# A decoder's l0 feed-forward prepared in one block, and its l1 selective scan laid out on 128 lanes

## The reference

```python
def _reorder_quantize_x(x, idx):                      # layer 0, feed-forward
    scale = jnp.max(jnp.abs(x)) / GLOBAL_DIV
    xr = (x / scale)[:, idx]
    scale_x = jnp.max(jnp.abs(xr), axis=1, keepdims=True) / FP8_MAX
    return (_fp8(xr / scale_x), scale_x, scale)
def _qlinear(qx, scale_x, scale, W, idx):
    Wr = W[:, idx]
    w_scale = jnp.max(jnp.abs(Wr), axis=1, keepdims=True) / FP8_MAX
    return qx * scale_x @ (_fp8(Wr / w_scale) * w_scale).T * scale
...
delta = jax.nn.softplus(delta_r @ dt_proj_W.T + dt_proj_b) * 0.001   # layer 1, attention
delta_A = jnp.exp(jnp.einsum('bld,dn->bldn', delta, A))               # n: 16 states, d: 96 channels
delta_B_u = jnp.einsum('bld,bln,bld->bldn', delta, Bp, u)
x = dA_t * x + dBu_t                                                  # over the 256 steps
y = jnp.einsum('bdn,bn->bd', x, C_t)                                  # ... + u * Dp
```

## Time and profile before

| | us |
|---|---|
| median of 3 runs (2959.87 to 2961.27) | 2960.64 |
| the profiled execution | 2961.07 |
| its span, first to last instruction | 2959.2 |
| l0 feed-forward, preparation (three blocks) | from 284 to 403.2 |
| l0 feed-forward, 8 tiles | 403.2 to 494.3 |
| layernorm ahead of l1 attention | 494.3 to 503.3 |
| l1 attention up to the scan | 503.3 to 578.1 |
| l1 scan and y out of PSUM | 578.1 to 704.1 |

### The profile page before, as it was taken

The page is one execution under the profiler, slowest core; times in us unless marked ns, Lnnn a source line. Parts: engine busy times, 40 slices in busy tenths (PEclk is TensorE's granted clock), DMA queues, the critical chain, the costliest instruction groups (busy, mean ns, idle before and its releaser), DMA issues. The chain is left out here.

```text
span 2959.2 us, 37118 instructions
## 1 busy us (share of the span) xinstructions
PE 2425.8 (82%) x14074; PEld 1610.9 (54%) x14074; DVE 1737.1 (59%) x3519; ACT 1008.2 (34%) x2293; POOL 769.9 (26%) x573
## 2 busy tenths in 40 slices
PE   7797343486999997977979797889998887999899
PEld 4555222123434555665858586755557765555555
DVE  5435678696435664278696969525665763565311
ACT  3032001362105552124545453415552131555210
POOL 1120001000007883300000000008881000888322
PEclk8788555697999998987888989789999969999999
DMA  1000000003000001041010101030001004000311
GB/s 35 19 21 22 0 0 14 0 0 107 1 0 1 1 1 58 1 147 27 30 29 30 29 30 29 2 100 1 1 1 43 21 1 100 1 1 1 118 36 39
DMA packets 98937, 81.29 MB, mean 27 GB/s; under 512 B 51504, under 2 KB 90272, under 8 KB 98185
## 3 DMA queue, kind: packets, MB, share of 16 engines
q1 hardware_dynamic: 97737, 77.47, 9.2%
q0 software_dynamic: 1024, 1.45, 0.2%
HBM read 73.56 MB, written 5.35 MB: 27 GB/s over the span
## 5 line engine op out<-in xcount | busy, mean ns | idle before, releaser
L2017 POOL TENSOR_SCALAR work<-work,small 128x512 f32<-128x512 f32 x384 | 594.3, 1566 | 706.6 <-DVE small L1952 705.3
L1995 ACT ACTIVATE work<-psum,small 128x512 f32<-128x512 f32 x384 | 260.6, 683 | 254.6 <-DVE small L1947 254.6
L1947 DVE TENSOR_REDUCE small<-psum 128x2 f32<-128x1024 f32 x192 | 234.7, 1224 | 176.0 <-PE psum L1897 176.0
L1907 PEld LDWEIGHTS psum<-consts,work 128*128 128x128 f32 x1536 | 165.4, 141 | 113.8 <-issue 102.1
L1897 PE MATMUL psum<-keysT,arena_a 64*128 64x512 f32 x768 | 219.2, 650 | 8.9 <-ACT work L1995 6.0
L1919 PE MATMUL psum<-work,keys 128*64 128x256 f32 x1536 | 187.0, 384 | 36.9 <-issue 34.3
L1907 PE MATMUL psum<-consts,work 128*128 128x128 f32 x1536 | 211.3, 281 | 3.5 <-DVE work L1958 2.6
L1919 PEld LDWEIGHTS psum<-work,keys 128*64 128x64 f32 x1536 | 120.0, 136 | 136.7 <-issue 110.8
L2849 PE MATMUL psum<-xnT,arena_a 128*128 128x256 f32 x512 | 138.2, 425 | 24.7 <-DVE arena_b L3269 23.8
L1958 DVE COPY work<-psum 128x512 f32<-128x512 f32 x192 | 130.9, 682 | 19.7 <-PE psum L1907 19.7
L2002 ACT ACTIVATE work<-psum 128x512 f32<-128x512 f32 x192 | 114.4, 596 | 71.8 <-PE psum L1907 71.8
(11 more groups left out here) (589 smaller groups left out, 4992.5 us busy)
## 6 DMA issues: line engine op xcount, KB each, us to landing
arena_b<-alpha_rows SPq DMA_DIRECT2D x16, 512.0 KB, 5.7
arena_a<-in_L_xattn_Wo SPq DMA_DIRECT2D x3, 2048.0 KB, 14.6
arena_a<-in_L_xattn_Wq SPq DMA_DIRECT2D x3, 2048.0 KB, 12.7
arena_a<-in_L_xattn_w_kc_q SPq DMA_DIRECT2D x3, 1536.0 KB, 12.2
arena_a<-in_L_attn_w_qkv SPq DMA_DIRECT2D x1, 4096.0 KB
arena_a<-in_L_xattn_W_qr SPq DMA_DIRECT2D x3, 768.0 KB
arena_b<-in_L_ffn_w_fc SPq DMA_DIRECT2D x1, 2048.0 KB
arena_b<-in_L_ffn_w_proj SPq DMA_DIRECT2D x1, 2048.0 KB
```

Source lines behind the costliest of these rows:

```text
L1907: mm = nc.tensor.transpose(ps[:, 4 + j, c * P:(c + 1) * P], probs[u % NPB][:, j, c * P:(c + 1) * P], k.c["ident"])
L1947: nc.vector.tensor_reduce(top[:, 2 * u:2 * u + 2], ps[:, u % 2 * 2:u % 2 * 2 + 2, :], AX.X, ALU.max, negate=True).then_inc(*maxed.up())
L1995: nc.scalar.activation(probs[u % NPB][:, j, :], ps[:, u % 2 * 2 + j, :], ACT.Exp, bias=top[:, i:i + 1], accum_out=total[:, i:i + 1]).then_ ...
L2017: nc.gpsimd.tensor_scalar(probs[u % NPB][:, j, :], probs[u % NPB][:, j, :], total[:, i:i + 1], None, ALU.mult).then_inc(*scaled.up())
```

## The change

In `l0_ffn` the first three blocks become one. The input is masked, reduced and rounded by DVE in the same instruction list as the weights, behind the weights' rounding. The row scales are spread by PE right after DVE has made them, into banks 3 to 7, and ACT copies them out. The permutation runs in two halves (`half`), each of 8 gate/up and 32 down matmuls, and ACT copies out both halves. The transposed and permuted input is copied out half by DVE and half by ACT. In the block over tiles `scale(t + 1)` now stands ahead of `hidden(t)`, the residual of a tile comes one turn later behind its hidden rows instead of two, and PE takes up the transposes of a tile two turns later.

In `l1_attn` the arrays of the step size and of the scan go from 96 partitions x 1024 to 128 partitions x (3 x 256): each batch has 32 partitions (`lane(b)`), and the 96 channels are three groups `j` of 32. `u` is brought into this layout by 12 transfers within the on-chip memory (`own_u`), and the three per-channel vectors and tables are loaded four times each, once for each batch. Operations with a per-partition scalar are issued once for each `j`. PE writes to 32 partitions at a time: `spread` has 8 matmuls of 256 columns per state (for 4 of 512) and `collect` 12 blocks of 32 x 32 (for 2 matmuls of 96 x 96), which also bring the sum back to 96 partitions.

```diff
...
             for i in range(4):
-                dve.wait_ge(*mm.at(1))
                 c, g = divmod(i, 2)
-                nc.vector.tensor_copy(qguT[:, c, g * F:(g + 1) * F], ps[:, 3 + i, :].bitcast(BF16)[:, 0:F])
+                last = nc.vector.tensor_copy(qguT[:, c, g * F:(g + 1) * F], ps[:, 3 + i, :].bitcast(BF16)[:, 0:F])
+            last.then_inc(*taken.up())
...
+            nc.vector.reciprocal(rx, sx).then_inc(*taken.up())
+            dve.wait_ge(*taken.at(2))
+            k.link(dve, nc.vector.tensor_scalar(rx, rx, FP8_MAX, None, ALU.mult), "dve")
+            k.link(dve, nc.vector.tensor_scalar(sx, sx, 1.0 / FP8_MAX, None, ALU.mult), "dve")
+            k.link(dve, nc.vector.tensor_tensor(xm, xm, rx.unsqueeze(2).broadcast_to([P, NT, D]), ALU.mult), "dve")
+            quantise(k, dve, xm, xt, qx)
+            nc.vector.tensor_copy(rx, rx).then_inc(*prep.up())
+            dve.wait_ge(*turned.at(1))
+            nc.vector.tensor_copy(qxT[:, 0, :], ps[:, 4, :].bitcast(BF16)).then_inc(*taken.up())
+            dve.wait_ge(*mm.at(6))
+            nc.vector.tensor_copy(xpick[:, 0, :].rearrange("p (a b) -> p a b", a=2), ps[:, 6:8, :])
...
+        @block.scalar
+        def _(act):
+            act.wait_ge(*rows_done.at(1))
             for i in range(4):
-                nc.vector.tensor_copy(scale_row[:, i * F // 2:(i + 1) * F // 2], ps[:, 4 + i, 0:F // 2])
+                nc.scalar.activation(scale_row[:, i * F // 2:(i + 1) * F // 2], ps[:, 4 + i, 0:F // 2], ACT.Copy)
+            nc.scalar.activation(scale_row2, ps[:, 3, 0:D], ACT.Copy).then_inc(*taken_act.up())
+            for half in range(2):
+                act.wait_ge(*mm.at(2 + 2 * half))
+                nc.scalar.activation(wpick[:, half, :].rearrange("p (a b) -> p a b", a=4), ps[:, 4:8, 0:F // 2],
+                                     ACT.Copy).then_inc(*taken_act.up())
+                act.wait_ge(*mm.at(3 + 2 * half))
+                nc.scalar.activation(wd_pick[:, 4 * half:4 * half + 4, :].rearrange("p (a b) d -> p a (b d)", a=2),
+                                     ps[0:FP, 2 * half:2 * half + 2, :], ACT.Copy)
+            act.wait_ge(*turned.at(2))
+            nc.scalar.activation(qxT[:, 1, :], ps[:, 5, :].bitcast(BF16), ACT.Copy).then_inc(*taken_act.up())
+            act.wait_ge(*mm.at(7))
+            nc.scalar.activation(xpick[:, 1, :].rearrange("p (a b) -> p a b", a=2), ps[:, 4:6, :], ACT.Copy)
...
             m.then_inc(*counted.up())
+            pe.wait_ge(*prep.at(2))
+            for t in range(16):
+                nc.tensor.matmul(ps[:, 4 + t // 4, t % 4 * FP:(t % 4 + 1) * FP], k.c["ones"][0:FP, :],
+                                 column(t, FP), start=True, stop=True)
+            for t in range(2):
+                m = nc.tensor.matmul(ps[:, 3, t * P:(t + 1) * P], k.c["ones"], column(16 + t, P), start=True, stop=True)
+            m.then_inc(*rows_done.up())
             pe.wait_ge(*prep.at(3))
+            pe.wait_ge(*taken_act.at(1))
...
+            for half in range(2):
+                pe.wait_ge(*(taken.at(1) if half == 0 else taken_act.at(2)))
...
+                m.then_inc(*mm.up())
+                if half == 0:
+                    pe.wait_ge(*taken.at(2))
+                for j in range(4 * half, 4 * half + 4):
+                    for t in range(FT):
+                        m = nc.tensor.matmul(ps[0:FP, j // 2, j % 2 * D:(j % 2 + 1) * D], pick_down[:, t, j * FP:(j + 1) * FP],
+                                             qdT[:, t, :], start=t == 0, stop=t == FT - 1)
+                m.then_inc(*mm.up())
+            pe.wait_ge(*prep.at(4))
+            pe.wait_ge(*taken_act.at(3))
...
-                if t >= 1:
-                    u = t - 1
+                if t >= 2:
+                    u = t - 2
...
-            for t in range(NT + 2):
+            scale(0)
+            for t in range(NT + 1):
+                if t + 1 < NT:
+                    scale(t + 1)
                 if t < NT:
-                    scale(t)
                     hidden(t)
-                if t >= 2:
-                    residual(t - 2)
+                if t >= 1:
+                    residual(t - 1)
...
+    G, J = P // B, C * B // P
...
-                                (cols[:, 0:1], col("L1_attn_conv_b", C)), (cols[:, 1:2], col("L1_attn_dt_proj_b", C)),
-                                (cols[:, 2:3], col("L1_attn_D_param", C)), (a_log, io["L1_attn_A_log"])])
+                                (conv_b, col("L1_attn_conv_b", C))]
+                 + [pair for b in range(B) for pair in (
+                     (a_log[lane(b)], io["L1_attn_A_log"].rearrange("(j g) n -> g j n", g=G)),
+                     (dt_b[lane(b)], col("L1_attn_dt_proj_b", G)), (skip[lane(b)], col("L1_attn_D_param", G)))])
...
-            nc.vector.tensor_scalar(conv.rearrange("p (a b) -> p a b", a=2), ps[0:C, 0:2, :], cols[:, 1:2], None,
-                                    ALU.add).then_inc(*k.sig("z").up())
+            for j in range(J):
+                last = nc.vector.tensor_scalar(z[:, j, :], ps[:, j // 2, j % 2 * S:(j % 2 + 1) * S], dt_b[:, j:j + 1], None, ALU.add)
+            last.then_inc(*k.sig("z").up())
...
-            nc.vector.tensor_tensor(du, delta, u, ALU.mult)
-            nc.vector.tensor_scalar(hC[1], u, cols[:, 2:3], None, ALU.mult)
+            dve.wait_ge(*laned.at(16 * B * J))
+            nc.vector.tensor_tensor(du, delta, own_u, ALU.mult)
+            for j in range(J):
+                nc.vector.tensor_scalar(hC[1][:, j, :], own_u[:, j, :], skip[:, j:j + 1], None, ALU.mult)
+
+        @block.sync
+        def _(sp):
+            sp.wait_ge(*silued.at(1))
+            for b in range(B):
+                for j in range(J):
+                    sp.dma_start(own_u[lane(b), j, :], u[G * j:G * j + G, b * S:(b + 1) * S]).then_inc(*laned.up(16))
...
-            for n in range(2):
-                mm = nc.tensor.matmul(ps[0:C, n, :], w_dt, low[:, n * 512:(n + 1) * 512], start=True, stop=True)
+            for j in range(J):
+                for b in range(B):
+                    mm = nc.tensor.matmul(ps[lane(b), j // 2, j % 2 * S:(j % 2 + 1) * S], w_dt[:, G * j:G * j + G],
+                                          low[:, b * S:(b + 1) * S], start=True, stop=True)
...
+            def spread(s):
+                if s >= 4:
+                    pe.wait_ge(*read.at(s - 3))
+                for g in range(2):
+                    at = R + g * NS + s
+                    for b in range(B):
+                        mm = nc.tensor.matmul(ps[lane(b), s % 4, g * S:(g + 1) * S], w_x[:, at:at + 1].broadcast_to([C, G]),
+                                              u[:, b * S:(b + 1) * S], start=True, stop=True)
                 mm.then_inc(*bred.up())
 
...
+                for d in range(B):
+                    for j in range(J):
+                        b = (j + d) % B
+                        mm = nc.tensor.matmul(ps[G * j:G * j + G, 4 + b, 0:S],
+                                              k.c["ident"][lane(b), lane(b)], hC[s % 2][lane(b), j, :],
+                                              start=s < 0, stop=s == NS - 1, skip_group_check=True)
...
-                k.link(act, nc.scalar.activation(dA[s % 2], delta, ACT.Exp, scale=a_log[:, s:s + 1]), "act")
-                nc.scalar.activation(ln_dA[s % 2], dA[s % 2], ACT.Ln, bias=k.c["tiny"][0:C]).then_inc(*decay.up())
+                for j in range(J):
+                    last = nc.scalar.activation(dA[s % 2][:, j, :], delta[:, j, :], ACT.Exp, scale=a_log[:, j, s:s + 1])
+                k.link(act, last, "act")
+                nc.scalar.activation(ln_dA[s % 2], dA[s % 2], ACT.Ln, bias=k.c["tiny"]).then_inc(*decay.up())
 
...
-                nc.vector.tensor_tensor(two(dBu[s % 2]), two(du), ps[0:C, b_at, :], ALU.mult).then_inc(*taken.up())
+                row = lambda g: ps[:, s % 4, g * S:(g + 1) * S].unsqueeze(1).broadcast_to([P, J, S])
+                dve.wait_ge(*bred.at(s + 1))
+                nc.vector.tensor_tensor(dBu[s % 2], du, row(0), ALU.mult).then_inc(*taken.up())
                 dve.wait_ge(*decay.at(s + 1))
-                k.link(dve, refine_exp(k, dve, dA[s % 2], delta, a_log[:, s:s + 1], ln_dA[s % 2]), "dve")
+                for j in range(J):
+                    own = ln_dA[s % 2][:, j, :]
+                    last = nc.vector.scalar_tensor_tensor(out=own, in0=delta[:, j, :], scalar=a_log[:, j, s:s + 1], in1=own,
+                                                          op0=ALU.mult, op1=ALU.subtract)
+                k.link(dve, last, "dve")
+                k.link(dve, nc.vector.scalar_tensor_tensor(out=dA[s % 2], in0=ln_dA[s % 2], scalar=1.0, in1=dA[s % 2],
+                                                           op0=ALU.add, op1=ALU.mult), "dve")
                 dve.wait_ge(*taken.at(s + 1))
-                for b in range(B):
...
+                for j in range(J):
```

(3 more changed lines are left out.)

144 lines of the change are left out of this document (39 added, 105 removed).

## The result

The changed kernel takes 2888.61 us (median of 4 runs, 2887.71 to 2889.92), the kernel before 2960.26 beside it (2958.35 to 2961.27). The ratio is 0.9758, with a 95% interval of 0.9744 to 0.9772: 71.7 us less, where 60.7 were forecast. The profiled execution took 2889.24 us, its span is 2887.4.

The account below looks back on a forecast made before the run. DVE was taken as the bound in l1_attn and the PE/DVE hand-over in l0_ffn's preparation. Terms -32.2 - 3.5 + 4.2 - 7.0 - 22.2 = -60.7 us gave a median of 2900.0, range 2888 to 2914.

Parts of the forecast that it names:

- l0 preparation: In l0_ffn ahead of the tiles: hand-over waits between PE and DVE go, first tile's matmul at 371.0, 32 us less.
- half of 3.86 us: In the l0 preparation: PE's time for each gate/up half, within 17.7 us for both halves of the permutation.
- by the row the sum stands: In the l0 preparation: PE's clock stays at 0.50 as in the old row, so the halves take 17.7 us.
- the first rival: TensorE's clock rises in the merged l0 block: 9 us less, 2891; chance 8%.
- Tiles: l0 tile loop: the 0.85 us tanh waits go, two new waits come; 3.5 us less.
- Loads: Layernorm ahead of l1: nine more loads issued by SP put all engines 4.2 us back; bound 7.5 us.
- l1 ahead of the scan: l1_attn before the scan: rows shrink from 1024 to 768 elements, and the w_dt product shortens; 7.0 us less.
- Scan: l1_attn scan: a step falls from 7.30 to 5.91 us, 22.2 us less over 16.
- the second rival: In the scan: ACT or PE becomes the bound, or short instructions cost more; 2917 or 2942; chance 13%.
- The last sum: End of the scan: the last collect, in the open, costs the same 3.4 us as now; bounds 0.9 to 10.2.
- The slower rival: In the scan: collect's 24 instructions go strictly one after another at 1.2 GHz, 11.9 us a step, 2996; chance 4%.
- the likeliest case: Whole kernel: the forecast schedule, median 2900.0, alone ranging from 2893 to 2909; the forecast keeps 75%.

Follow-up runs that it names:

- e7_by_rows: The changed kernel with the 12 blocks of each collect issued batch by batch instead of along diagonals; 2888.66 us, ratio 0.9758.
- late loads: The changed kernel with l1 attention's twelve per-lane loads issued in the next block; 2891.31 us, ratio 0.9745, and again 2884.53 us, ratio 0.9748.
- e2_l1_only: The new l1_attn with the old l0_ffn, against the kernel before; 2930.43 us, ratio 0.9909.
- e5_before_fill: The kernel before with 200 unread matmuls put in PE's idle time ahead of the rounded weights; 2966.37 us, ratio 0.9994.
- e9_picks_first: The changed kernel with both gate/up halves first, then all 64 down matmuls in one run; 2897.70 us, ratio 0.9768.

## Why the prediction was right, and where it was short

The sign, the main mechanism and the order of the terms were right; the time lies near the low edge of the range, since the spans differ by 71.8 us where the sum had 60.7, 11.1 us more. Term by term:

- **l0 preparation, -32.2 forecast, -37.8 measured.** The schedule was right: with the second down half at the first's 7.03 us (3.06 more), the input's transposes at 1.89 (0.83 more) and its permutation at 3.60 (1.71 more; both the earlier trace rows) the measured 90.27 us become 95.9, and the forecast's 128.08 - 32.2 is 95.9. Inside it two errors cancel: "half of 3.86 us" is short for a half at 0.50, because the clock was up for the end of that row; the two whole halves would have taken 18.3 us at 0.50 for the 17.7 forecast, and PE started 0.55 us sooner than forecast. The step that failed is "by the row the sum stands": the 0.50 of the old 14 us did not carry over. This is the first rival, in part: the clock rose, but at 357.8 and not at 345, so it gave 5.6 of its 9 us. The Trainium skill, "TensorE: Matmul & The Clock Gate", Part 1 (The HAM clock gate), has sustained work raise the clock. The trace after agrees (unbroken work from 345.61, the rise at 357.8); the 64 matmuls of before, 13.88 us at 0.50, do not, and in `e7_by_rows` the clock fell within unbroken work, near 347.3.
- **Tiles, -3.5 forecast, -5.9 measured.** The waits came as forecast but one: none for tanh, 2.87 us at the end (2.9 forecast), and 1.46 us at the start (2.5 forecast). The two first products ran at 1.35 and 1.37 us for 2.50 since the clock was still high. That is some 2.3 us of the same cause, and the shorter wait at the start is 1.0 of them.
- **Loads, +4.2 forecast, +4.4 measured** (5.04 for 0.64), SP last as forecast. The late loads undo just this term. The bound of 7.5 us was taken from an issue of 0.80 us as the slowest, but the issue before it in that list, of `in_kv_cos`, took 1.11 us already then (1.47 after); the new loads took 0.43 each, so nothing hung on it.
- **l1 ahead of the scan, -7.0 forecast, -7.3 measured.** The reciprocal was 4.95 us for 6.55, in proportion to its elements.
- **Scan, -22.2 forecast, -21.8 measured.** The step is 5.92 for 5.91 forecast. Three exps of 256 take 1.31 us, 0.44 each, so ACT's round of 4.86 us stays under DVE's, ACT waits for DVE's scan (1.07 us a step) as forecast, and the second rival has no row that speaks for it. That the clock fell to 0.50 in the scan (the low-clock price had been worked out) costs nothing that shows in a step.
- **The last sum, 0 forecast, -2.5 measured.** The mis-sized term: `collect` was put at 3.4 us, three blocks at a time, and is 1.14. A pass of 256 columns at this clock is half of the 0.85 us that 512 take; 24 of them one by one would be 10.2 us, so by this estimate some nine of the twelve blocks run at once. The row of before that answers to 632.96 is

```profile
702.86 1.22 DVE L1552 COPY arena_b<-psum 96x1024 f32<-96x1024 f32 x1 [3.82 <-PE psum L1511]
```

  with 3.82 us of waiting for 1.33. The slower rival (blocks strictly in turn) falls with the same row, and no drain between tiling modes is seen: `spread` begins 1.07 us after the collect does (548.77 and 549.84), and DVE waits for neither.
- **The rest, 0 forecast, -0.9 measured.** The attention of layer 2, which nobody touched, is 2.9 us shorter. It is not the change: over the twelve later profiles it is 656.9 to 657.8 us in seven and 659.8 to 660.2 in five, the unedited changed kernel's second profile (660.02) and the kernel before with fillers (660.19) among the latter. Other parts move as well, and more: over all profiles the first part takes 121.8 to 128.0 us and the second 140.2 to 151.0, though no edit touches them.

Two small sums of the forecast are off without consequence. ACT's round passes 5.91 us at 0.81 us an exp, (5.91 - 2 x 1.28 - 0.92) / 3, and not at 0.79; and the bounds of the likeliest case add up to 2894 and 2908, not 2893 and 2909.

In one place the chances were too sharp: the clock had 8%, on a single row. That row is of a stretch with 3.3 us of idle ahead of it, and the change takes such idle times away; the rival's own argument said so, and was weighed too low. In the kernel before the clock did fall inside one of these idle times, between 352 and 352.8, having been at 1.00 until then: the row priced at 0.50 stood behind a clock that had been up. In `e2_l1_only`, which has the same l0, it was at 1.00 from 349 to 350 as well and the 64 took 13.88 us again. That the idle time is what took it down is argued, not shown.

What stays open: why the 64 matmuls of before stay at 1.2 GHz through 13.88 us of unbroken work, in all three profiles of that order (the kernel before, `e5_before_fill`, `e2_l1_only`), while the same 64 run at 2.4 GHz nearly throughout in `e9_picks_first`; and how much of the tile order's 4.7 us comes out in time.
